# Recurrent attention with a routed expert layer in one fp32 kernel: beginning reordered, biases and part of the output sums moved to TensorE

## The reference

```python
xn = layernorm(x)
q = silu(xn @ Wq);  k = l2_norm_per_head(silu(xn @ Wk));  v = xn @ Wv       # 16 heads of 16
log_f = log_sigmoid(xn @ Wf1 @ Wf2);  gamma = -sigmoid(xn @ Wgamma)
a = k * gamma * exp(log_f)
# recurrence over 512 steps, a 16 x 16 state S per sequence and head
S = S * exp(log_f_t);  S = S + k_t * (a_t . S + v_t);  o_t = q_t . S
o = o * sigmoid(xn @ Wog1 @ Wog2);  s = layernorm(o) * norm_w @ Wo
# experts: E = 8, two chosen per token, DFF = 1024
w = softmax(xn @ Wg + bg);  top two, divided by their sum + 1e-8
y = sum over the two of weight * (gelu(xn @ W1[e] + b1[e]) @ W2[e] + b2[e])
g = silu(layernorm(y) * gamma + beta)
out = x + s * g
```

## Time and profile before

| | us |
|---|---|
| median of 3 runs | 1197.97 (1197.68 to 1198.45) |
| the profiled execution | 1202.44 |
| its span | 1200.7 |
| VectorE busy | 1101.2 (92%) |
| TensorE busy | 924.2 (77%) |
| GpSimd busy | 923.5 (77%) |
| ScalarE busy | 412.9 (34%) |

### The profile page before, as it was taken

How to read it: one execution, slowest core, us unless ns; L and a number is a source line. 1 busy time by engine, 2 the same in 40 slices (tenths; PEclk the granted TensorE clock), 3 DMA queues, 4 the chain that set the end, 5 groups by cost and what they waited for, 6 DMA issues and landing times.

```text
span 1200.7 us, 17400 instructions
## 1 busy us (share of the span) xinstructions
PE 924.2 (77%) x3777; PEld 678.7 (57%) x3778; DVE 1101.2 (92%) x3401; ACT 412.9 (34%) x1113; POOL 923.5 (77%) x912
## 2 busy tenths in 40 slices
PE   5888988410007999999999999999999996676761
PEld 2333433100005777877777878888787885555550
DVE  3789999989999999999999989989999999999995
ACT  3444454300002332223333223332223331687861
POOL 3766666628771888888888878888888888899883
PEclk9788898755557999999999999999999998688885
DMA  5565666466243666656665656666666653566322
GB/s 161 177 217 178 187 208 190 142 167 187 78 116 101 203 190 182 199 172 198 206 180 187 187 173 193 177 191 205 184 184 202 201 171 100 161 174 181 104 74 62
DMA packets 238035, 202.60 MB, mean 169 GB/s; under 512 B 140401, under 2 KB 216017, under 8 KB 237969
## 3 DMA queue, kind: packets, MB, share of 16 engines
q1 hardware_dynamic: 160930, 82.81, 26.2%
q10 hardware_dynamic: 70224, 100.49, 25.6%
q0 software_dynamic: 6816, 18.69, 4.7%
HBM read 139.42 MB, written 62.54 MB: 168 GB/s over the span
## 4 chain that ended last, share of the span: by engine, by line
PE 48%; DVE 17%; POOL 16%; issue 7%; DMA 6%; SPq 3%; ACT 1%; ACTq 0%; DVEq 0%; POOLq 0%
PE psF L941 22%; PE psA L929 20%; POOL xs_d L522 6%; PE psF L943 4%; POOL prod_a L330 3%; DMA rec_d<-work 3%; POOL prod_q L347 2%; DMA work<-xs_d 2%; DVE obh L1223 2%; SPq L355 2%; DVE ubuf L1239 1%; DVE prod_a L1234 1%; DVE work L1067 1%; PE psT L917 1%; DVE work L1082 1%
## 5 line engine op out<-in xcount | busy, mean ns | idle before, releaser
L330 POOL TENSOR_TENSOR prod_a<-state,rbh 128x512 f32<-128x512 f32 x200 | 254.6, 1273 | 95.1 <-DVE state L1294 69.8
L941 PE MATMUL psF<-wts,work 128*128 128x256 f32 x1248 | 290.9, 386 | 3.8 <-ACT work L732 2.7
L929 PE MATMUL psA<-xT,wts 128*128 128x256 f32 x1248 | 282.4, 385 | 0.8 <-ACT xT L726 0.8
L941 PEld LDWEIGHTS psF<-wts,work 128*128 128x128 f32 x1248 | 231.9, 191 | 51.6 <-issue 17.0
L929 PEld LDWEIGHTS psA<-xT,wts 128*128 128x128 f32 x1248 | 235.5, 191 | 45.1 <-issue 13.8
L347 POOL TENSOR_TENSOR prod_q<-state,rbh 128x512 f32<-128x512 f32 x175 | 222.1, 1269 | 0.0
L1223 DVE TENSOR_REDUCE obh<-prod_q 128x16 f32<-128x272 f32 x512 | 217.9, 426 | 0.0
L732 ACT ACTIVATE work<-psA,b_sb 128x256 f32<-128x256 f32 x312 | 131.1, 471 | 162.0 <-PE psA L929 161.9
L743 ACT ACTIVATE work<-psF,work 128x256 f32<-128x256 f32 x78 | 37.0, 474 | 262.4 <-PE psF L943 258.6
L1283 DVE TENSOR_REDUCE ubuf<-prod_a 128x16 f32<-128x272 f32 x200 | 86.1, 430 | 36.1 <-POOL prod_a L330 35.9
L917 PE MATMUL psT<-ident,work 128*128 128x128 f32 x156 | 24.4, 280 | 118.6 <-DMA work<-xs_d 118.5
(11 more groups left out here) (178 smaller groups left out, 1518.2 us busy)
## 6 DMA issues: line engine op xcount, KB each, us to landing
wts<-in_L_ffn_W_dram ACTq DMA_DIRECT2D x78, 1024.0 KB, 5.6
rec_d<-work SPq DMA_DIRECT2D x32, 768.0 KB
rbh<-rec_d SPq DMA_DIRECT2D x32, 768.0 KB, 5.8
xs_d<-zero SPq DMA_DIRECT2D x26, 387.0 KB, 9.4
work<-xs_d ACTq DMA_DIRECT2D x39, 258.0 KB, 5.7
wts<-y_d ACTq DMA_DIRECT2D x16, 512.0 KB, 6.3
x_acc<-in_L_attn_x_dram SPq DMA_DIRECT2D x32, 128.0 KB
o_d<-obh SPq DMA_DIRECT2D x32, 128.0 KB, 7.9
```

The source lines that it names most:

```text
L330: eng.tensor_tensor(prod_a[:, n, 1:3, :, 0:HD], state[:, g % SR, :, :].unsqueeze(1).broadcast_to(wide), rows.unsqueeze(2).broadcast_to(wid ...
L929: mm = pe.matmul(psA[m // 2 % 2][:, m % 2 * MT:(m % 2 + 1) * MT], w1_sb[v][:, c, m * P:(m + 1) * P], xgT[:, c, :], start=(c == 0), stop=(c ...
L941: pe.matmul(psF[q][:, 0:D], hT[:, m, q * P:(q + 1) * P], w2_sb[v][:, m, :], start=(m == 0), stop=False)
```

## The change

Seven edits, all inside one program:

- Beginning: `STATS` starts with a group of one tile. Loads of x are spread between the weights and the first spills; constants are loaded behind the third spill, b2 behind the seventeenth.
- Records: ScalarE evaluates Silu itself, straight into the record, and its order is changed to groups of two tiles (both Silus and squares, then both tiles' sigmoids). The router's bias comes from a one-row matmul, and ScalarE copies the logits. VectorE's `silu` and the bias addition are gone. GpSimd's `factors` takes the norm first.
- Routing: works on differences from the largest logit, with fewer steps, one scan in place of eight, and pairs of steps that don't wait for each other.
- Output sums: for the rows in `SUMMED` (64 to 94) `sum_row` does nothing; TensorE sums 17 columns of eight rows at a time into psB by multiplying with the identity, and `gate_outputs` reads psB. The products go to a region of `work`, and `read_found` comes behind the new state.
- Sharing with GpSimd begins at pair 53 (`SWITCH`) instead of 56.
- Biases: b2 leaves the experts. The gate weights times the biases are added in the output stage, one matmul of 32 rows per token tile. L943 is gone.
- The table of row writes: `LAND_STEP` 14.9 for 15.9, `LAND_LAG` 12, and no write before pair 57.

```diff
-STATS = ((0, 4), (4, 8), (8, 16), (16, 24), (24, 32))
+STATS = ((0, 1), (1, 4), (4, 8), (8, 16), (16, 24), (24, 32))
+SWITCH = 53
+SUMS = 32, 48
+SUMMED = range(2 * SUMS[0], 2 * SUMS[1] - 1)
-LAND0, LAND_STEP = 390.0, 15.9
+LAND0, LAND_STEP, LAND_LAG = 390.0, 14.9, 12.0
...
+                if n == 0:
+                    load_x(4)
                 if n < RB:
                     sp.wait_ge(s_recd[n % RS], 16)
                     load_chunk(n, n)
+                if n == 0:
+                    load_x(5)
+                if n == 2:
+                    load_constants()
...
-            pool.wait_ge(s_sc, 32 * NT)
...
-            for g in range(SHARED * NP, T // 2):
+            for g in range(SWITCH, T // 2):
                 products(g)
-                ready = LAND0 + landed // MH * LAND_STEP
+                ready = LAND0 + LAND_LAG + landed // MH * LAND_STEP
...
+            def silu_kq(n):
+                u, u4 = n % 2, n % RS
+                act.wait_ge(s_A, n + 1)
+                if n >= RS:
+                    act.wait_ge(s_recd[u4], n // RS * 16)
+                act.activation(rec[:, u4, :, K_:K_ + 2 * HD].rearrange("p h (s c) -> p s h c", s=2),
+                               psA[u][:, :].rearrange("p (s h c) -> p s h c", s=2, h=H), ACT.Silu).then_inc(s_kq, 1)
...
+            for group in [(0,)] + [(n, n + 1) for n in range(1, NT - 1, 2)] + [(NT - 1,)]:
+                for n in group:
+                    ahead(n)
+                    silu_kq(n)
+                for n in group:
+                    sigmoids(n)
...
+                pe.matmul(psB[u][:, D + H:D + H + E], ones[0:1, :], bg_bc[0:1, :], start=False, stop=True).then_inc(s_Bp, 1)
...
-                    pe.matmul(psF[q][:, 0:D], ones[0:1, :], b2_flat[:, bass.ds(e * D, D)], start=False, stop=True)\
-                        .then_inc(s_y, 1)
+            for m in range(SUMS[0] // 4, SUMS[1] // 4):
+                at = (4 * m - SUMS[0]) * 2
+                pe.wait_ge(s_chain, (4 * m + 4) * CHAIN + 1)
...
+                for k in range(ROW):
+                    mm = pe.matmul(q_sums[:, at:at + NP, :], ident[:, :], q_rows[:, 8 * m % RING:8 * m % RING + NP, :, k],
+                                   start=(k == 0), stop=(k == ROW - 1))
+                mm.then_inc(s_ro, 1)
...
+                    pe.matmul(sums[j % 2][:, n % 2 * D:(n % 2 + 1) * D], denseT[:, n // 4, :], b2_sb[:, n % 4, :],
+                              start=True, stop=False)
...
-                dve.tensor_tensor(rec[:, u4, :, K_:K_ + 2 * HD].rearrange("p h (s c) -> p h s c", s=2), sides(psA[u][:, :]),
-                                  sides(sg[:, u, :]), ALU.mult).then_inc(s_kq, 1)
-                dve.tensor_tensor(logits[:, n, :], psB[u][:, D + H:D + H + E], bg_bc[:, :], ALU.add).then_inc(s_lg, 1)
...
-                for e in range(E):
-                    link(dve.tensor_tensor_scan(cum[:, :, e], ones[:, 0:NT], tot[:, :, e], 0.0, ALU.mult, ALU.add))
+                link(dve.tensor_tensor_scan(upto, scan_keep[:, :, :].rearrange("p e t -> p (e t)"), counted, 0.0, ALU.mult, ALU.add))
...
                 row = 2 * g - 1 + side
+                if row in SUMMED:
+                    return
```

More of the change, by code:

```diff
@@ L749, in expert_tile @@
                     load_rows(t + 2, v)
+            act.wait_ge(s_dT, 1)
+            for n in range(2):
+                act.activation(denseT[:, 4 * n:4 * n + 4, :], psA[n][0:4 * E, :].rearrange("p (n t) -> p n t", t=P),
+                               ACT.Copy).then_inc(s_dTs, 1)
             for t in range(2):
@@ L1099, in route, with step, link @@
                 done = [0]
-                def link(ins):
+                def step(ins):
                     ins.then_inc(s_dG, 1)
                     done[0] += 1
+                def link(ins):
+                    step(ins)
                     dve.wait_ge(s_dG, done[0])
-                ex, pr, m1, rest_, m2 = (gw[:, i, :, :] for i in range(5))
+                chosen, far, m1, rest_, m2 = (gw[:, i, :, :] for i in range(5))
                 dve.wait_ge(s_lg, NT)
@@ L1126, in route @@
[L1126 to L1131 removed]
+                first_of_largest(far, 3, m1)
@@ L1230, in two_steps @@
                 done = g * CHAIN + 1
-                if tile is not None and tile < NT:
-                    silu(tile)
                 dve.wait_ge(s_chain, done)
```

312 lines of the change are left out of this document (186 added, 126 removed).

## The result

| | before | changed |
|---|---|---|
| first timing, median of 5 (lowest to highest) | 1197.98 us (1197.68 to 1199.68) | 1204.51 us (1203.16 to 1206.08) |
| ratio | | 1.0047, 95% interval 1.003 to 1.0065 |
| the same two kernels on chip 15, medians | 1200.12 us | 1185.86 us (1183.39 to 1187.02); ratio 0.9884 (0.9856 to 0.9913) |
| and on chip 9 | 1198.36 us | 1205.96 us (1203.67 to 1212.97); ratio 1.0068 (1.0045 to 1.0091) |

The forecast was 1160 us (1151 to 1173), with a chance of 0.03 for slower. The first timing is slower by 0.5%. The kernel before takes nearly the same on every chip (medians 1198.0 to 1201.6), the changed one does not: on some chips VectorE stands still in pair 47, for 14.1 to 17.8 us, on others it doesn't. "First timing" is the run of the result above, whose chip is one that stops; which chip it was is not known.

The account below looks back on a forecast made before the run. VectorE's recurrence chain was taken to bound, the experts nearly level. Gains of 2.5 + 11.1 + 5.3 + 10.1 + 2.6 + 6.6 = 38.2 took the profiled 1202.44 to 1164.2, less 4.5 to the median: 1160 us, range 1151 to 1173.

Parts of the forecast that it names:

- D: Output sums, pairs 34 to 49: 31 rows move from VectorE to TensorE, 10.1 us gained, 0 to 1 lost at pair 47.
- rival 4: Pairs 44, 47 and 55: VectorE waits for TensorE's sums or the scatters, up to 5 each; 1166 to 1172, chance 0.06.
- A: Beginning, up to pair 3: earlier start mostly spent waiting for record 3's landing; 2.5 us gained.
- the 23 of the prediction: Beginning: record 0 put at 23 us, so its spill leaves 8 earlier than at 31.38.
- The end named for a loss: Beginning: the worst case, a loss of 4 us, with record 3's landing at 78.
- G: Output stage: one more matmul per token tile, 19 us on TensorE, covered by its idle time; nothing gained or lost.
- B: Record pairs 8 to 27: two instructions leave VectorE, 13.6 us, less 2.5 of stalls; 11.1 gained.
- the mark of 6.2: Record pairs 8 to 27: the forecast is wrong if they take over 6.2 us each.
- Rivals 2 and 5: Record stage: ScalarE or TensorE paces, 1167 or 1172, chance 0.15; a landing-bound loop over three tiles makes it slower, 1220, 0.03.
- C: Routing: fewer steps and one scan for eight, 18.6 us down to 13.3, a gain of 5.3.
- E: Sharing with GpSimd from pair 53: three pairs get shorter, 2.6 us gained.
- F: Experts: tiles every 15.1 us instead of 16.4, so GpSimd's row-write waits go; 6.6 us gained.

Follow-up runs that it names:

- again: The changed kernel word for word, run again on chip 15: 1185.86 us, no stop in pair 47.
- again_b: The changed kernel itself once more, on chip 9, which stops: 1205.96 us.
- nobias: The changed kernel without TensorE's 32 matmuls of the routing weights with b2 at the end, so the output lacks b2: 1196.79 us on chip 6.
- best: zeros with TensorE's output projections of two tiles put ahead of the expert-row sums and bias of two later pairs of tiles: 1191.32 us on chip 10.
- late: best with the gate of chunk 4 in pair 52 instead of pair 47: 1183.97 us on chip 9.
- x5: The changed kernel with the second group of x loads issued behind the second record's spill, not ahead of it: 1187.33 us on chip 13.
- zeros: The changed kernel with second x loads and constants issued later, and stores of zeros beginning after the fifth spill: 1195.34 us on chip 6.
- hold: The changed kernel with GpSimd waiting for TensorE's fourth group of sums before the second half of the scatters: 1211.98 us on chip 10.
- late0: The changed kernel with the gate of chunk 4 in pair 52, and TensorE's fourth group not waiting for it: 1196.68 us on chip 9.

## Why the prediction was wrong, step by step

**Pair 47 (D, rival 4).** The failed step: "34 passes take 11.7 [...] the gate in pair 47 reads the third group 11.6 after it began: 0 to 1 lost". A group took 8.0 on chips that don't stop, and the third 29.3 where the chip stops. Rival 4 had the place, with 5 us; I priced the duration of the work (11.7 at the low clock, for the 8.0 measured at a mean of 0.69 from 300 to 330) and never the delay of its signal. No row of before could show that, since TensorE did nothing while scatters were in flight; I bounded the matmuls, not the new dependence. On a chip that doesn't stop D came out at 9.4 for 10.1.

**A, beginning.** The failed step: "the spill leaves at some 64 and lands 8 to 10 later". It left at 71.87 and landed at 81.2. The mis-sized term is "two groups of eight loads (5 each)". From spill 0 to spill 3 the queue took 46.6 us for the 31.1 of before, 15.5 more, where the 64 of the prediction had 9.2 more. The second group of x took 10.35, and the stretch in which it stands, from the first chunk load to spill 1, is 9.1 longer than before (35.03 to 46.50 for 38.91 to 41.29) where the sum had 5. The first group, 9.06, lies under the wait for landing 0 and makes it 2.2 longer, which was put at nothing. The stretch with the constants is 4.3 longer, for 4.2. The rest is spill 0 itself, 2 later than the 23 of the prediction. The landing took 9.3, as priced. Instead of 2.5 gained, 7.4 to 8.3 were lost. The end named for a loss was 4. What the prediction said would be seen, an idle time over 4.87 in pair 3, was seen: 9.37.

**G, end.** The failed step: "Nothing; without that cover a few us". The idle time of TensorE was there (36% of this stage before, by the stretch above), and was no cover: VectorE waited 6.3 to 16.0 us (again, again_b), 4.6 to 5.4 net in the two profiles above, 11.9 in again_b. nobias and best show both cause and cure: the bias stood in TensorE's order ahead of a projection that VectorE needed at once. The work itself was near its price, 16 us in best for the 19.

**B, record pairs.** The mis-sized term: "some 0.68 of 6.55 per pair", less 2.5 of stalls. Pairs 8 to 27 took 6.25 each (6.19 on chip 15) for 6.58, at the mark of 6.2 that the prediction had set itself. Pairs without chunk work took 5.67 and 5.78 for 6.22 and 6.29: 0.53 less, not 0.68. Two of VectorE's steps grew (from 131 to 147, L368 takes 488 ns for 418, L1342 332 for 247), beside a ScalarE that went from 14.27 to 23.46 busy of 30 and a GpSimd from 19.73 to 24.40; and 2.4 us went to waits for GpSimd's factor (1.4 on chip 15). That the busier engines make the steps longer no run shows. Rivals 2 and 5 did not come: VectorE has 30.00 busy of 30 from 120 to 150. The table load stayed 1.28 to 1.29 from its start to the next instruction (20.06 to 21.35), as in the earlier trace rows. By the 2.66 of the Trainium skill (ScalarE: Activation LUTs, What ACT_TABLE_LOAD costs) ScalarE would, by estimate, have been full here; it was 78% busy, so the measured 1.28 holds.

**C, E, F** held: 4.8 for 5.3; 2.1 for 2.6; 6.0 to 6.2 for 6.6. The scan over 256 took 0.69. For F, no row write waits for a copy any more (rows above, against 6.6 in the earlier trace rows), the tiles came every (976.8 - 412.7) / 37 = 15.2 for the 15.1 forecast, and the last ended 45 ahead of pair 219, for 50.

Chip 15, which doesn't stop, is the fair test of the sum, and the forecast fails there too: 18.7 gained in the profiled execution, 14 in the medians, for 38.2. A is 10.8 of the difference, G 4.6, B 2, the others 2. What stays open is which property of chips 6, 9 and 10 delays the signals, and whether the kernel before meets it there; its times (1198.4 to 1201.1) say that it loses nothing by it.

Open too is whether the stop belongs to the kernel or to its recording. Every time here comes with a span and a granted clock, so every execution was recorded in some way, and the late signals came only on chips where records are missing, though not every signal is late where they are. The Trainium skill (NOTIFIC — the notification-queue block, 7.1 Overflow: three behaviours, one of which stalls the engine) says that inside this block a record is not lost but holds up what made it, and that under one of the block's policies new records are dropped when the ring in memory is full; an engine may so be slowed by its own records. No run here tells that from another cause: an execution without any record is not among them.

## What to carry to other kernels

A term that makes one engine wait for another's new work needs two prices, that of the work and that of the signal at that moment; put the reader of a new result behind the burst of transfers (late), or give the gain up: here, on chips that stop, the 10 us of sums were worth less than their stop. Time a change on more than one chip: here the sign of the whole hung on it. A queue with waits on landings is priced by what stands behind each wait, one landing at a time, and taking one transfer out lets the next one take its place (x5). And the idle share of an engine is no cover, not even that of the stage where the work goes: ask what stands behind the new work in that engine's order, and who waits for it (zeros against best).

## What was not expected of the hardware

The same program took 1185.9 us on one chip and 1206.0 on another, both times against a kernel before of 1198 to 1200. On three numbered chips and that of the first timing TensorE's semaphore update came 20 to 22 us late (28.2 to 29.9 for 8.0) while GpSimd's scatters were in flight, and not with them held back (hold); on chip 9, where nobody waited at the gate, VectorE's own came 1.0 to 5.5 us late each (late0, late). The end of a matmul that a trace draws is modelled: here it was 21 us too early, and the semaphore's update told the truth.
